# A two-layer sequence model on one core: readouts one scan later, ScalarE's side work behind both decays of a pair, the D term from ScalarE, a closed order of state tiles

## What is computed

```
xz = xn @ in_proj.T; x_in, z = split(xz)               # xn: layernorm, scaled and shifted by cond
u  = silu(conv4(x_in) + conv_b)                        # 1024 channels
dt_r, B, C = split(u @ x_proj.T); dt = softplus(dt_r @ dt_proj.T + b)
h[t] = h[t-1] * exp(dt[t] * A) + (dt[t] * u[t]) * B[t] # 1024 channels x 16 states, t = 0..127
y[t] = sum_n h[t] * C[t] + u[t] * D_param
x    = x + gate * ((y * silu(z)) @ out_proj.T)
```

## Time and profile before

| | us |
|---|---|
| median of 3 runs | 4975.43 |
| the profiled execution, its own time | 4976.74 |
| its span, first to last instruction | 4975.0 |
| granted TensorE clock over the span | 0.976 |

### The profile page before, as it was taken

One profiled execution on the slowest core, in us unless ns is written; L12 is line 12 of the kernel. 1 busy time (PEld: TensorE's weight loads), 2 busy tenths in 40 slices (PEclk: granted clock), 3 DMA queues, 4 the chain that ended last, 5 costly groups with the idle time before them and its releaser, 6 DMA issues. The chain is left out here.

```text
span 4975.0 us, 74942 instructions
## 1 busy us (share of the span) xinstructions
PE 4419.1 (89%) x21856; PEld 3161.0 (64%) x21856; DVE 4137.6 (83%) x5011; ACT 3129.7 (63%) x7557; POOL 4010.7 (81%) x1861
## 2 busy tenths in 40 slices
PE   7898888888898989888888888898976999999998
PEld 4666666666666666666666666666654666565664
DVE  2999999999999999999999999999993656566664
ACT  2777777777777777777777777777761333333332
POOL 0999999999999999999999999999992333334332
PEclk9999999999999999999999999999988999999999
DMA  5111111111111111111111111111103323222221
GB/s 193 39 43 46 43 46 43 44 52 52 62 46 44 46 44 46 44 43 44 54 57 58 43 44 46 44 46 43 43 35 112 101 84 100 84 100 79 97 87 45
DMA packets 121581, 301.58 MB, mean 61 GB/s; under 512 B 15394, under 2 KB 20770, under 8 KB 120675
## 3 DMA queue, kind: packets, MB, share of 16 engines
q1 hardware_dynamic: 121186, 296.91, 17.6%
HBM read 245.35 MB, written 51.51 MB: 60 GB/s over the span
## 5 line engine op out<-in xcount | busy, mean ns | idle before, releaser
L635 POOL TENSOR_TENSOR dbu<-du,bc 128x1024 f32<-128x1024 f32 x1024 | 2406.8, 2383 | 111.2 <-DVE du L573 111.2
L396 ACT ACTIVATE dA<-dt,c_A 128x256 f32<-128x256 f32 x4096 | 1753.5, 467 | 524.4 <-DVE hC L539 392.4
L602 DVE TENSOR_TENSOR_SCAN hS<-dA,dbu 128x512 f32<-128x512 f32 x1024 | 1205.4, 1208 | 176.1 <-PE Y L277 123.6
L646 POOL TENSOR_TENSOR hS<-hS,bc 128x1024 f32<-128x1024 f32 x512 | 1220.0, 2383 | 62.7 <-DVE hS L602 62.7
L602 DVE TENSOR_TENSOR_SCAN dA<-dA,dbu 128x512 f32<-128x512 f32 x1024 | 1208.5, 1212 | 20.8 <-ACT dA L396 15.0
L277 PEld LDWEIGHTS Y<-c_ident,hC 128*128 128x128 f32 x4096 | 481.0, 144 | 284.6 <-DVE hC L539 190.2
L277 PE MATMUL Y<-c_ident,hC 128*128 128x128 f32 x4096 | 556.2, 280 | 116.1 <-DVE hC L539 112.1
L539 DVE TENSOR_TENSOR hC<-dA,bc 128x1024 f32<-128x1024 f32 x512 | 627.0, 1225 | 22.4 <-DVE dA L602 5.7
L318 PE MATMUL side<-c_in_w,xnF 128*128 128x512 f32 x1024 | 509.1, 621 | 94.0 <-DVE u L565 55.5
L277 PE MATMUL Y<-c_ident,hS 128*128 128x128 f32 x4096 | 548.9, 278 | 16.1 <-POOL hS L646 16.1
L335 PE MATMUL side<-xnF,c_in_w 128*128 128x256 f32 x2048 | 491.4, 384 | 73.8 <-DVE zs L560 49.1
(11 more groups left out here) (125 smaller groups left out, 5668.5 us busy)
## 6 DMA issues: line engine op xcount, KB each, us to landing
bc<-b_scratch SPq DMA_DIRECT2D x256, 512.0 KB, 3.8
x_in<-in_x SPq DMA_DIRECT2D x32, 512.0 KB, 5.2
o_scratch<-oS SPq DMA_DIRECT2D x64, 256.0 KB, 2.0
p_o_in<-o_scratch SPq DMA_DIRECT2D x32, 512.0 KB, 4.8
p_g_in<-gate_scratch SPq DMA_DIRECT2D x32, 512.0 KB, 5.8
p_x<-in_x SPq DMA_DIRECT2D x32, 512.0 KB, 6.4
x_scratch<-p_x_in SPq DMA_DIRECT2D x32, 512.0 KB, 3.2
p_xr<-x_scratch SPq DMA_DIRECT2D x32, 512.0 KB, 6.8
```

The lines of the kernel that those rows point to most:

```text
L396: last = act.activation(dA[:, q % A_RING, e, :], dt[j % 2][:, e, :], ACT.Exp, scale=C["A"][:, 2 * j + e, n:n + 1])
L602: dve.tensor_tensor_scan(out.rearrange("p e t -> p (e t)"), dA[:, q % A_RING, :, :].rearrange("p e t -> p (e t)"), dbu[(q // 2) % B_RING][ ...
L635: gps.tensor_tensor(dbu[p % B_RING][:, :, :, :], du[j % 2][:, :, :].unsqueeze(1).broadcast_to([P, 2, 2, GT]), bc[:, 0, n:n + 2, :].unsquee ...
L646: gps.tensor_tensor(h, h, bc[:, 1, n:n + 2, :].unsqueeze(2).broadcast_to([P, 2, 2, GT]), ALU.mult).then_inc(hcP_done, 1)
```

## The change

- `KINDS` becomes a list of four equal strings, with counts by quarter; the kinds and counts stay as they are.
- VectorE's readout of D pair p moves from behind scan 2p + 1 to behind scan 2p + 2 (in the next group for the last pair). D_ACC, G_ACC, YZ_AT, YT_AT, YF_AT and DMM_AT move with it.
- ScalarE does all four decay instructions of a pair and then the side work of both slots.
- The D term: ScalarE writes uD = u * D_param (two 128x256 activations for each quarter) into a new tile, and TensorE adds it by transposing matmuls against the identity; the diagonal matrices and the eight instructions that made them go.
- The hS tiles get an explicit table S_SLOT, with one shift at quarter 1 and one at quarter 3, which makes the order closed over a group: 0 1 2 0, 2 0 1 2, 0 1 2 0, 2 0 1 2. hC keeps i modulo 3.
- du = dt * u gets a slot of its own behind the softplus' last step; XN's copies are split in two halves; side items get new slots.

```diff
-def slot_free(i, ring, n):
-    if i >= ring:
-        return i - ring + 1
-    return max(k for k in range(n) if k % ring == i) + 1 - n
+def slot_free(i, table):
+    n = len(table)
+    return next(k for k in range(i - 1, i - 1 - n, -1) if table[k % n] == table[i]) + 1
...
-D_ACC = [8, 11, 15, 17]
-G_ACC = [7, 10, 14, 17]
+D_ACC = {4: [8, 12, 16, 18], 5: [8, 10, 12, 16, 18]}
+G_ACC = {4: [7, 11, 14, 17], 3: [5, 12, 17]}
...
-    ("Z", 1, 0, [3, 4, 5, 5]),
-    ("XI", 2, 1, [7, 8, 8, 9]),
-    ("O", 0, -1, [9, 10, 12, 13, 13, 14, 14, 15]),
-    ("CV", 1, 1, [16, 16, 18, 18]),
-    ("DT", 2, 0, [18]),
-    ("XI", 3, 1, [19, 20, 20, 21]),
...
+    ("Z", 1, 0, [2, 3, 5, 6]),
+    ("XI", 2, 1, [8, 8, 9, 9]),
+    ("O", 0, -1, [10, 10, 11, 11, 12, 13, 13, 14]),
+    ("CV", 1, 1, [15, 15, 17, 17]),
+    ("DT", 2, 0, [21]),
+    ("XI", 3, 1, [25, 26, 27, 28]),
...
-    ("XN", 0, 2, [48]),
+    ("XN", 0, 2, [44]),
...
-    ("CV", 0, 2, [57, 58, 59, 60]),
+    ("CV", 0, 2, [57, 59, 60, 61]),
...
-DT_COPY = 6
+DU_AFTER, DT_COPY = 5, 7
-YZ_AT = [18, 34, 50, 66]
-YT_AT = [20, 36, 52, 68]
-YF_AT = [22, 38, 54, 70]
-DMM_AT = [6, 22, 38, 54]
-Q_STATS, Q_AGGR, Q_RSTD, Q_NMR, Q_XHAT = 34, 35, 38, 40, 42
+YZ_AT = [19, 35, 51, 67]
+YT_AT = [19, 36, 52, 68]
+YF_AT = [22, 36, 55, 69]
+DMM_AT = [7, 23, 39, 55]
+UD_AT = [1, 17, 33, 49]
+Q_STATS, Q_AGGR, Q_RSTD, Q_NMR, Q_XHAT = 28, 31, 34, 35, 38
+S_SLOT = [(G_BASE[j] + i + sum(j >= at for at in (1, 3)[:-NGP % S_RING])) % S_RING for j in range(4) for i in range(len(G_PAIRS[j]))]
...
     skip_term, TensorE
-            wait(pe, u_done, g * 4 + (j + 1))
+            wait(pe, uD_done, g * 4 + (j + 1))
...
-                    last = pe.matmul(Y[:, b, k * P:(k + 1) * P], u[par][:, 2 * j + k, b * P:(b + 1) * P],
-                                     W["skip"][:, 2 * j + k, :], start=(b == 0 and k == 0), stop=False, skip_group_check=True)
+                    last = pe.matmul(Y[:, b, k * P:(k + 1) * P], uD[:, k, b * P:(b + 1) * P], C["ident"][:, :],
+                                     start=(b == 0 and k == 0), stop=False, is_transpose=True, skip_group_check=True)
...
     ScalarE
+        def skip_values(g, j, par):
+            wait(act, u_done, g * 4 + (j + 1))
+            wait(act, dmm_done, g * 4 + j)
+            for k in range(2):
+                last = act.activation(uD[:, k, :], u[par][:, 2 * j + k, :], ACT.Copy, scale=C["dcol"][:, 2 * j + k:2 * j + k + 1])
+            last.then_inc(uD_done, 1)
...
+            for q in range(0, UNITS, 2):
+                if inside(at, 0):
+                    for i in range(2):
+                        bank_freed(act, g, q + i)
...
+                        decay(g, q + i, 0)
+                        decay(g, q + i, 1)
+                beside(q)
+                beside(q + 1)
...
     VectorE
-                    if KINDS[p] == "D" and half == 1:
-                        readout(g, j, D_PAIRS.index(p))
+                    for m, p in enumerate(D_PAIRS[j]):
+                        t = 16 * j + 2 * p + 2
+                        if q == t % UNITS and inside(at, -(t // UNITS)):
+                            readout(g - t // UNITS, j, m)
...
     setup
-        for e in range(KI):
-            dve.tensor_scalar(W["skip"][:, e, :], C["ident"][:, :], C["dcol"][:, e:e + 1], None, ALU.mult)
```

More of the change, by code:

```diff
@@ L102 @@
 S_RING = 3
+C_SLOT = [i % C_RING for i in range(ND)]
+S_SLOT = [(G_BASE[j] + i + sum(j >= at for at in (1, 3)[:-NGP % S_RING])) % S_RING for j in range(4) for i in range(len(G_PAIRS[j]))]
 PAIRS = UNITS // 2
@@ L132, in mamba @@
     hC = [sb(f"hC{i}", [P, 2, 2, GT]) for i in range(C_RING)]
+    uD = sb("uD", [P, 2, GT])
     zs = sb("zs", [P, GB, D])
@@ L204, in bank_freed @@
         j, p = old // NST, old % NST // 2
-        if KINDS[p] == "D":
-            wait(eng, hcD_done, go * 4 * ND + (j * ND + D_PAIRS.index(p) + 1))
+        if KINDS[j][p] == "D":
+            wait(eng, hcD_done, go * ND + (D_BASE[j] + D_PAIRS[j].index(p) + 1))
         else:
@@ L398, in decay, with simple @@
                 last.then_inc(dA_ready, 1)
-        def simple(kind, j, src, own, par):
+        def simple(kind, j, src, own, par, part):
             wait(act, filled[kind], nth(kind, j, own))
@@ L404, in simple @@
                 wait(act, filled["Z"], own * 4 - 4)
[L405 to L410, removed]
+                for b in range(GB):
+                    k, s = 2 * j + part, (part * GB + b) * P
+                    last = act.activation(xnF[par][:, k, b * P:(b + 1) * P], src[:, s:s + P], ACT.Identity,
+                                          scale=C["gm0"][:, bass.ds(own * GB + b, 1), k], bias=C["bm0"][:, bass.ds(own * GB + b, 1), k])
+                if part == 1:
+                    last.then_inc(xn_done, 1)
             elif kind == "XI":
@@ L480, in stages, with beside @@
                         staged(kind, j, stage, bank[bk], tmp[(sig_base[of] + s) % 2], go + d, earlier(2, s, of, go, sigs_at))
[L482 to L491, removed]
+            def beside(q):
+                stages(q, 2, S2)
+                stages(q, 1, S1)
                 stages(q, 0, 0)
@@ L495, in body @@
                         copy_dt(j, bank[bk], go + d)
-                    if kind in ("XN", "XI", "XP", "O") and q == end + A_AFTER[kind] - off:
-                        simple(kind, j, bank[bk], go + d, (of + d) % 2)
+                    for part in range(2 if kind == "XN" else 1):
+                        if kind in ("XN", "XI", "XP", "O") and q == end + A_AFTER[kind] + 2 * part - off:
+                            simple(kind, j, bank[bk], go + d, (of + d) % 2, part)
                 for j in range(4):
+                    if q == UD_AT[j] and inside(at, 0):
+                        skip_values(g, j, at % 2)
                     t = YF_AT[j]
@@ L561, in side_dve @@
             elif kind == "CV":
-                wait(dve, dmm_done, own * 4 - 8 + (j + 1))
+                wait(dve, uD_done, own * 4 - 8 + (j + 1))
                 wait(dve, filled["XP"], own - 1)
@@ L570, in side_dve, with step_times_u @@
                 dve.scalar_tensor_tensor(src[:, :], src[:, :], 0.0, t[:, :], ALU.max, ALU.add).then_inc(dt_done, 1)
[L571 to L574, removed]
+        def step_times_u(j, src, own, par):
+            wait(dve, dt_done, own * 4 + (j + 1))
+            wait(dve, dbu_ready, own * PAIRS + 8 * (j - 1))
+            dve.tensor_tensor(du[j % 2][:, :, :].rearrange("p e t -> p (e t)"), src[:, :],
+                              u[par][:, 2 * j:2 * j + 2, :].rearrange("p e t -> p (e t)"), ALU.mult).then_inc(du_done, 1)
         def work(at, off):
@@ L594, in body @@
                     p, half = n // 2, n % 2
-                    if KINDS[p] == "D":
+                    if KINDS[j][p] == "D":
                         out = dA[:, q % A_RING, :, :]
                     else:
-                        i = j * NGP + G_PAIRS.index(p)
+                        i = G_BASE[j] + G_PAIRS[j].index(p)
                         if half == 0:
-                            wait(dve, yP_done, g * 4 * NGP + slot_free(i, S_RING, 4 * NGP))
-                        out = hS[i % S_RING][:, half, :, :]
+                            wait(dve, yP_done, g * NGP + slot_free(i, S_SLOT))
+                        out = hS[S_SLOT[i]][:, half, :, :]
                     dve.tensor_tensor_scan(out.rearrange("p e t -> p (e t)"), dA[:, q % A_RING, :, :].rearrange("p e t -> p (e t)"),
@@ L619, in body @@
                 for (kind, j, d, end, bk, s, off), of, go in side:
+                    if kind == "DT" and q == end + DU_AFTER - off:
+                        step_times_u(j, bank[bk], go + d, (of + d) % 2)
                     if kind in D_AFTER and q == end + D_AFTER[kind] - off:
@@ L652, in body @@
                 for j in range(4):
-                    for m in range(NGP):
-                        t = 8 * j + G_PAIRS[m] + G_LAG
+                    for m in range(len(G_PAIRS[j])):
+                        t = 8 * j + G_PAIRS[j][m] + G_LAG
                         if p == t % PAIRS and inside(at, -(t // PAIRS)):
@@ L1255, in program @@
             for name, shape in (("in", [P, KD, 2 * DI]), ("x", [P, KI, XD]), ("dt", [XD + 1, DI]),
-                                ("out", [P, KI, D]), ("conv", [P, KI, TAPS, P]), ("skip", [P, KI, P])):
+                                ("out", [P, KI, D]), ("conv", [P, KI, TAPS, P])):
                 const(layer0, W, name + "_w", shape)
```

80 lines of the change are left out of this document (43 added, 37 removed).

## The result

The changed kernel takes 4917.93 us (median of 4, 4916.33 to 4919.17) against 4975.59 us: ratio 0.9883, interval 0.9866 to 0.9900, so 1.2% or 57.7 us faster. The forecast was 4912 us. The profiled execution took 4919.17 us, its span is 4917.4 us.

A forecast was written before the change was run, and what follows sets the result against it. GpSimd was taken to bound mamba, with VectorE right behind. Terms of -58.6, -4.0 and -1.4 sum to -64.0 us against 4976.7, so 4912.7 us profiled and 4912 us as the median; range 4902 to 4948.

The forecast's parts named there:

- The bound and the floor: In mamba GpSimd is the limit, 111.37 us a group, 3564 us over 32 groups; its idle time is 62.7 us.
- Closed order: At group boundaries VectorE's wait at scan 0 goes, and with it GpSimd's waits at loop ends: 58.6 us gained.
- 0 to 2: Four tiles a group reused after two G pairs: cost 0, or up to 2 us each if TensorE is held up.
- 14 waits: GpSimd's waits before readouts, one for each turn of the hardware loop: 58.6 us, 4.19 on average.
- The loop's end: Where the loop branches, TensorE's 2.91 us standstill falls beside VectorE's last scans; even 2 us at `gate_y` wouldn't reach GpSimd.
- Start: Setup and first scan: -1.65 us without diagonals, -1.9 from an earlier first scan, -0.4 from split XN copies; -4.0 us.
- End: Before the last gate the G pair's accumulation now comes ahead of the D pair's: -1.4 us.
- VectorE's balance: VectorE may wait 6.4 us a group before becoming the bound, 1.6 of it from later readouts; forecast about 2.
- Under 2 us a group: Sign in the profile after: VectorE's wait for ScalarE stays under 2 us a group.
- Side work behind both decays: ScalarE's side work ahead of slots freed by readouts: new stalls under 1 us a group.
- D term: ScalarE's eight copies a group, 3.7 us taken, are hidden, as it has 83.4 of 111.4 us in use.
- about equal for TensorE: In the D term sixteen matmuls a group become sixteen transposes, about equal for TensorE, which is no bound.

The follow-up runs named there:

- run 1: The kernel before with the closed order of hS tiles and nothing else: 4925.54 us, ratio 0.9894.
- run 2: The changed kernel with its hS tiles in the old order, i modulo 3: 4959.73 us, ratio 0.9965.
- Run 3: The kernel before with four groups instead of two in a turn of the hardware loop: 4955.64 us, ratio 0.9956.
- run 7: The changed kernel with VectorE's readouts back directly behind their scans, accumulations and gates at their new slots: 4917.42 us, ratio 0.9880.
- run 8: The changed kernel with ScalarE's old lacing, a sigmoid stage between the halves of each slot's decays, side work behind each slot: 4991.75 us, ratio 1.0028.
- run 9: The changed kernel with XN's first transposes back at slot 48, behind XP: 4931.62 us, ratio 0.9909.
- run 6: The changed kernel with the old D term, matmuls of u against diagonals: 4918.59 us, ratio 0.9883.
- run 4: The kernel before with the new D term alone, ScalarE copies and transposes, no diagonals: 5001.04 us, ratio 1.0052.
- run 12: The changed kernel with five D pairs in quarter 3 and the old D term: 4896.21 us, ratio 0.9830.
- run 10: The changed kernel with one G pair of quarter 3 turned into a D pair, so five D pairs there: 4870.79 us, ratio 0.9786.

## Why the prediction was right

- **The bound and the floor.** "GpSimd is the limit", 111.37 us a group without waits: it is 111.3 now. The gain is its 62.7 us of waits, of which 61.2 went.
- **Closed order, -58.6 us.** Right as a sum, and runs 1 and 2 show that the tiles carry most of it: 50 to 53 us alone, 42 in the changed kernel; the last 5 to 8 come from the rest of the change. Run 3 shows the share of the loop's turning. The tiles reused after two pairs cost VectorE 17.4 us, 0.5 us once a group and 1.8 in two places, within my "0 to 2", and GpSimd nothing. I had counted "14 waits" as one for each turn; they are 13 and a short one at the loop's entry, which leaves the sum as it is.
- **The loop's end.** "TensorE thus turns round while VectorE still does its last scans": its standstill is seen only once in the profile after, and GpSimd waits at no loop's end. The rule of the Trainium skill on taken branches ("Runtime: NRT & Kernel Launch", "Instruction fetch mechanics") agrees in that the standstill doesn't go: what VectorE meets is ScalarE's, 2.99 us in the turn shown where it had 1.67, or its own, which I had not counted.
- **Start, -4.0 us.** The term that failed: the first readout is 1.05 us sooner. Without the diagonals mamba begins 1.15 us sooner (first memset at 56.02 instead of 57.17 us), and ScalarE's decays come right behind the convolution's first step, as I said. But XN's transposes now stand between the pieces of XP, B's values are stored 1.3 us later, and `scale_b` begins at 115.31 us instead of 113.79, released by the load of B. The first scan starts at 123.70 us, not 122.9. I looked at slot 44 in the steady groups only. **End, -1.4 us**: it was 0.6 us more from GpSimd's last readout to the last gate. The sum gave 4912.7 us for the profiled execution, which took 4919.17. Start and end fell short by 3.0 and 2.0 us, and the stretch behind the last gate, for which I had no term, gave 3.5 back; GpSimd's slightly faster pace made up 2.0 of it, which I had not foreseen and which is luck.
- **VectorE's balance.** 1.6 us a group from the later readouts: run 7 shows 1.56 (50.0 us less of waits for GpSimd without them, in 32 groups). Waits for ScalarE: I said about 2 us a group, it is 3.1; so 2.8 us of slack are left where 4.4 were forecast, and it waits for GpSimd in 101 places, not in hundreds. Before it was 7 places, not 5: I had left out the two before hS scans. "Under 2 us a group" for ScalarE, one of my signs, thus did not come true, though the time did.
- **Side work behind both decays, "under 1 us a group"** of new stalls: a little too low (waits for ScalarE rose from 59.5 to 100.0 us, 1.3 a group). What I did not see is how much hangs on ScalarE's order: with the old lacing the same kernel is at 4992 us (run 8), and with one item of side work two pairs later at 4932 (run 9).
- **D term, "this is hidden".** Right in the changed kernel (run 6), for a reason that I had not given: on the kernel before it costs 23 us (run 4), where VectorE hardly ever waited for GpSimd and so had no slack to give. That one part was right by luck: my argument, that ScalarE is busy only 83.4 of 111.4 us, holds for the kernel before as well. An engine that is busy 75% can still be on the path in bursts. The transposes are not "about equal for TensorE" either: they take 0.60 us a quarter where the matmuls against the diagonals took 1.05, which changed nothing, as TensorE is no bound.
- **Not tried by themselves:** du's own slot, the split XN copies and the new slots of the other side items.

## What to carry to other kernels

When two engines are within a few per cent of each other, price a part by the slack that it takes from the second, not by the first: here the D term cost 23 us, 3 us or nothing, and with five D pairs it gained 25 (run 12 against run 10), and five D pairs gave 47 us or 22, according to what else was left of VectorE's slack. Look where a ring of buffers closes over a loop: a ring that doesn't divide the count can make one reuse immediate, and here it fell where the loop's branch stalls. And once the bound engine shows no wait at all, give its work to the other until the waits of the two meet: one instruction a group moved gave 47 us where the whole change had given 58.

## What was not expected of the hardware

Where the loop branches back, several engines stand still with no releaser, each by its own time, which differs from turn to turn: TensorE for 2.69 to 3.77 us and ScalarE for 1.41 to 1.76 in the kernel before, ScalarE for 2.98 to 3.12 in the four turns of the changed kernel that show it, for 2.00 to 3.89 in run 10 and 2.10 to 3.87 in run 12; VectorE is idle for 1.80 us with no releaser in the turn shown. Once VectorE waits for ScalarE, TensorE's idle time of 3.58 us is followed by matmuls at half pace (0.9 us each instead of 0.47, granted clock 0.50), which carries the delay through to a second wait of 3.47 us, 13 us later; behind 3.11 us of idle time in run 10 the clock stayed at 1.00.
